# Attention and feed-forward layers in pairs of blocks, with the probabilities divided ahead of the value matmuls

## The reference, cut to what matters

```
x = attn_layer(shift_tokens(x), Wqkv[i], ...) + x      # 16 heads of 64
x = ffn_layer(shift_tokens(x), ...) + x                # 128 -> 2 * 341 -> 128
```

## Time and profile before

| | us |
|---|---|
| median of 3 runs | 1887.88 |
| lowest and highest run | 1884.1, 1891.57 |
| the profiled execution's own time | 1885.08 |
| its span in the trace | 1882.9 |
| TensorE busy (matmul) | 1716.6 (91%) |
| VectorE busy | 1664.4 (88%) |
| ScalarE busy | 1363.7 (72%) |
| GpSimd busy | 1289.6 (68%) |

### The profile page before, as it was taken

The page is one execution under the profiler, slowest core; times in us unless marked ns, Lnnn a source line. Parts: engine busy times, 40 slices in busy tenths (PEclk is TensorE's granted clock), DMA queues, the critical chain, the costliest instruction groups (busy, mean ns, idle before and its releaser), DMA issues. The chain is left out here.

```text
span 1882.9 us, 83647 instructions
## 1 busy us (share of the span) xinstructions
PE 1716.6 (91%) x33456; PEld 1329.2 (71%) x33456; DVE 1664.4 (88%) x3697; ACT 1363.7 (72%) x2647; POOL 1289.6 (68%) x724
## 2 busy tenths in 40 slices
PE   3947899999999999999999999999999999999984
PEld 2524677777777777777777777777777777777773
DVE  5788889999999999899999899999899999999975
ACT  3334678777777877877777787787777778778762
POOL 1538767777767777777777677777677777777741
PEclk8878999999999999999999999999999999999996
DMA  3001222222322222322212322222321222222220
GB/s 133 1 1 46 81 69 58 53 67 78 91 65 67 54 58 78 102 54 67 67 48 75 111 53 59 67 60 62 111 65 49 64 67 68 66 67 59 53 68 23
DMA packets 80680, 121.62 MB, mean 65 GB/s; under 512 B 16776, under 2 KB 29574, under 8 KB 79750
## 3 DMA queue, kind: packets, MB, share of 16 engines
q1 hardware_dynamic: 80646, 121.14, 24.1%
HBM read 19.36 MB, written 1.05 MB: 11 GB/s over the span
## 5 line engine op out<-in xcount | busy, mean ns | idle before, releaser
L1174 POOL TENSOR_TENSOR rot<-rot,root 128x1024 f32<-128x1024 f32 x192 | 365.3, 1903 | 392.3 <-DVE root L1048 392.3
L716 PE MATMUL r<-wqkv,xs 128*128 (+1 forms) x1152 | 528.6, 595 | 5.3 <-ACT xs L879 3.9
L1159 POOL TENSOR_TENSOR rot<-rot,rot_sin 128x1024 f32<-128x1024 f32 x192 | 451.2, 2373 | 0.0
L902 ACT ACTIVATE squares<-r 128x512 f32<-128x512 f32 x384 | 229.0, 597 | 298.1 <-PE r L716 295.2
L716 PEld LDWEIGHTS r<-wqkv,xs 128*128 128x128 f32 x1152 | 205.0, 191 | 194.6 <-issue 187.2
L1010 DVE TENSOR_TENSOR rot_sin<-r,table 128x512 f32<-128x512 f32 x384 | 245.3, 679 | 0.0
L1005 DVE TENSOR_TENSOR rot<-r,table 128x1024 f32<-128x1024 f32 x192 | 234.0, 1219 | 12.5 <-ACT squares L902 8.4
L1166 POOL TENSOR_TENSOR squares<-squares 128x512 f32<-128x512 f32 x192 | 241.6, 1281 | 0.6 <-ACT squares L902 0.4
L721 PE MATMUL r<-square,rot 128*128 128x128 f32 x1536 | 206.0, 279 | 36.1 <-DVE rot_sin L1010 30.4
L1179 POOL TENSOR_TENSOR sm<-sm,rowmax 128x1024 f32<-128x1024 f32 x96 | 182.6, 1902 | 65.7 <-DVE rowmax L1058 65.7
L721 PEld LDWEIGHTS r<-square,rot 128*128 128x128 f32 x1536 | 172.0, 143 | 58.5 <-DVE rot_sin L1010 50.8
(11 more groups left out here) (131 smaller groups left out, 3165.1 us busy)
## 6 DMA issues: line engine op xcount, KB each, us to landing
vwin<-vtok SPq DMA_DIRECT2D x576, 128.0 KB
vwin<-vtok SPq DMA_DIRECT2D x384, 64.0 KB
wqkv<-in_wqkv SPq DMA_DIRECT2D x6, 1536.0 KB, 6.3
wo<-in_wo SPq DMA_DIRECT2D x6, 512.0 KB, 3.9
w<-in_w SPq DMA_DIRECT2D x6, 341.0 KB, 3.0
x<-in_x SPq DMA_DIRECT2D x4, 256.0 KB, 3.7
rope<-in_rope SPq DMA_DIRECT2D x1, 1024.0 KB
out_x<-y SPq DMA_DIRECT2D x4, 256.0 KB, 2.3
```

The source lines that it names most:

```text
L716: pe.matmul(dst[:, c * 512:(c + 1) * 512], xs1[:, u, 0:P], w.rearrange("p a n -> p (a n)"), start=True, stop=True).then_inc(S[done], 1)
L902: last = act.activation(squares[:, k, c * 512:(c + 1) * 512], src[:, c * 512:(c + 1) * 512], ACT.Square)
L1159: pool.tensor_tensor(r, r, rot_sin[:, k, :, :, :].rearrange("p h a d -> p h (a d)"), ALU.add)\
L1174: pool.tensor_tensor(r, r, bcast(root[:, k * HEADS:(k + 1) * HEADS], 2, DH), ALU.mult)\
```

## The change

A step now takes a pair of blocks, m = 0 to 47, and each engine's order within a step is new.

- Four blocks of values are kept in `vtok`, and `vwin`, `qT`, `sm`, `probs`, `rinv` and `pT` have a copy for the even and the odd block.
- `find_roots` serves a pair: 64 sums of squares, one column that is only filler, and two variances, 67 columns; the first operation works on 65.
- VectorE divides the probabilities (`weigh`) ahead of their transposition. In `attend` the values are stationary (64 rows, 64 columns) and the probabilities move (32 columns); the result has features on partitions, so ScalarE copies it straight into `attnT`. The eight transpositions and the division of the attended values are gone.
- Output projection, centring, norm, gate and down projection work on 256 tokens. The up projection comes in three pieces, one for each part of the 341 rows, placed apart in the orders. The variance and the spreading of its root take two matmuls a pair each.
- The first residual is written by one operation into a tile of its own, `mid`, with a column of zeros ahead of each sequence; ScalarE makes the shifted copy `xs2` from it (`stage2`, two operations). `xT` has such a column as well, and the carried columns are gone.
- ScalarE loads the tables for GELU and for the exponential once a pair.
- On SyncE the loads of `w1` and `w2` come after all four spreadings at a layer's end, that of `wo` ahead of them.

The diff, cut to its core. In `step` of TensorE the waits that guard the reuse of PSUM are left out; ScalarE's step is left out.

```diff
+PAIRS = STEPS // 2
+PPL = NB // 2
+PPB = BPB // 2
+W2 = 2 * P
...
-ROOTS = 2 * HEADS + 1
+QK_ROOTS = 4 * HEADS
+ROOTS = QK_ROOTS + 3
...
+        ss = sb("ss", [P, QK_ROOTS + 1])
+        qT = sb("qT", [P, 2, FT, P])
+        vtok = sb("vtok", [P, 4 * INNER])
+        vwin = sb("vwin", [P, 2, NW, FT, DH])
+        sm = sb("sm", [P, 2, HEADS, 2 * WIN])
+        probs = sb("probs", [P, 2, HEADS, 2 * WIN])
+        rinv = sb("rinv", [P, 2, HEADS])
+        pT = sb("pT", [P, 2, FT, P])
+        attnT = sb("attnT", [P, FT, W2])
+        mid = sb("mid", [P, BATCH * (SEQ + 1)])
+        xc = sb("xc", [P, 3, W2])
+        gate = sb("gate", [P, 3, W2])
+        hid = sb("hid", [P, 3, W2])
...
+        LAG, FILLED, BEHIND = 2, 6, 4
...
+            for m in range(FILLED):
+                step(m)
+            with eng.Fori(FILLED, PAIRS) as m:
+                step(m)
+            for m in range(PAIRS, PAIRS + BEHIND):
+                step(m)
...
+                pairs = sp.snap(PPL * (layer + 1))
+                pieces = sp.snap(3 * PPL * (layer + 1))
+                following = sp.snap(layer + 1)
+                sp.wait_ge(S["wo_done"], pairs)
+                weights.load_wo(sp, following)
                 spread_v(used, 0)
-                sp.wait_ge(S["wo_done"], used)
-                weights.load_wo(sp, layer + 1)
                 spread_v(used + 1, 1)
                 spread_v(used + 2, 0)
-                sp.wait_ge(S["up_done"], used)
-                weights.load_w1(sp, layer + 1)
                 spread_v(used + 3, 1)
-                sp.wait_ge(S["down_done"], used)
-                weights.load_w2(sp, layer + 1)
+                sp.wait_ge(S["up_done"], pieces)
+                weights.load_w1(sp, following)
+                sp.wait_ge(S["down_done"], pairs)
+                weights.load_w2(sp, following)
             with sp.Fori((STEPS - NB) // 2 + 2, STEPS // 2) as j:
...
+            def turn_probs(n, u, dst):
+                pe.wait_ge(S["weighted"], n + 1)
+                transpose_all(dst, probs[:, u, :, :].rearrange("p h k -> p (h k)"), "pT_done")
...
+            def attend(n, u, dst):
                 pe.wait_ge(S["pT_copied"], n + 1)
+                pe.wait_ge(S[f"v_spread{u}"], SPREADS * (n // 2 + 1))
                 pe.sem_inc(S["attend_begun"], 1)
                 for i in range(FT // 2):
+                    for w in range(NW):
+                        for s in range(2):
+                            for e in range(2):
+                                half = slice(2 * WIN * e, 2 * WIN * (e + 1))
                                 rows = slice(WIN * w, WIN * (w + 1))
+                                at = 512 * e + P * i
+                                last = pe.matmul(dst[DH * s:DH * (s + 1), at + WIN * w:at + WIN * (w + 1)],
+                                                 vwin[half, u, w, 2 * i + s, :],
+                                                 pT[half, u, (FT // 2) * s + i, rows], start=True, stop=True)
+                last.then_inc(S["attended"], 1)
...
+            def out_project(m):
+                pe.wait_ge(S["attnT_copied"], 2 * (m + 1))
+                pe.wait_ge(S["wo_loaded"], 16 * (m // PPL + 1))
                 for f in range(FT):
+                    last = pe.matmul(pm_out[:, 0:W2], wo[:, f, :], attnT[:, (f % 2) * (FT // 2) + f // 2, :],
+                                     start=(f == 0), stop=(f == FT - 1))
                 last.then_inc(S["wo_done"], 1)
...
+            def ff_up(m, t, dst):
+                if t == 0:
+                    pe.wait_ge(S["xn2_ready"], m + 1)
+                    pe.wait_ge(S["w1_loaded"], 16 * (m // PPL + 1))
+                at, rows = FFT[t]
                 for half in range(2):
+                    last = pe.matmul(dst[0:rows, half * W2:(half + 1) * W2],
+                                     w1[:, half * FF + at:half * FF + at + rows], xn2[:, :], start=True, stop=True)
                 last.then_inc(S["up_done"], 1)
...
+            def step(m):
+                if runs(m - 2):
+                    attend(2 * m - 4, 0, r1)
+                if runs(m - 4):
+                    ff_up(m - 4, 1, pm_out)
+                if runs(m):
+                    project(2 * m, 0, 1, r0, "k_proj")
+                if runs(m - 3):
+                    spread_rstd(m - 3)
+                if runs(m - 1):
+                    turn_k(2 * m - 2, 0, r1)
+                if runs(m - 2):
+                    turn_probs(2 * m - 3, 1, r2)
+                if runs(m - 4):
+                    pe.wait_ge(S["gated"], 3 * (m - 4) + 2)
+                    ff_up(m - 4, 2, pm_out)
+                if runs(m - 1):
+                    pe.wait_ge(S["kT_copied"], 2 * m - 1)
+                    turn_q(2 * m - 2, 0, r1)
+                if runs(m - 2):
+                    attend(2 * m - 3, 1, r2)
+                if runs(m - 1):
+                    score(2 * m - 2, 0, r1)
+                if runs(m):
+                    pe.wait_ge(S["k_turned"], 3 * (2 * m + 1))
+                    project(2 * m, 0, 0, r0, "q_proj")
+                if runs(m - 1):
+                    turn_k(2 * m - 1, 1, r2)
+                if runs(m - 2):
+                    out_project(m - 2)
+                if runs(m - 1):
+                    pe.wait_ge(S["kT_copied"], 2 * m)
+                    turn_q(2 * m - 1, 1, r2)
+                if runs(m):
+                    pe.wait_ge(S["q_turned"], 3 * (2 * m + 1))
+                    project(2 * m + 1, 1, 0, r0, "q_proj")
+                if runs(m - 1):
+                    pe.wait_ge(S["masked"], 2 * m - 1)
+                    score(2 * m - 1, 1, r1)
+                if runs(m):
+                    project(2 * m + 1, 1, 1, r2, "k_proj")
+                    project(2 * m, 0, 2, r1, "v_proj")
+                if runs(m - 4):
+                    ff_down(m - 4)
+                if runs(m - 2):
+                    ff_center(m - 2)
+                if runs(m - 1):
+                    turn_probs(2 * m - 2, 0, r1)
+                if runs(m):
+                    pe.wait_ge(S["q_turned"], 3 * (2 * m + 2))
+                    project(2 * m + 1, 1, 2, r0, "v_proj")
+                if runs(m - 2):
+                    ff_var(m - 2)
+                if runs(m - 3):
+                    ff_up(m - 3, 0, r2)
...
+            def find_roots(m):
+                before = ROOT_OPS * m
+                if runs(m):
+                    dve.wait_ge(S["q_summed"], 2 * (m + 1))
+                    dve.wait_ge(S["k_summed"], 2 * (m + 1))
+                    dve.tensor_scalar(minus_half[:, 0:QK_ROOTS + 1], ss[:, :],
                                       1e-24, -0.5, ALU.max, ALU.mult)\
+                       .then_inc(S["refined"], 1 if runs(m - LAG) else 2)
+                if runs(m - LAG):
+                    dve.wait_ge(S["var_done"], m - LAG + 1)
+                    dve.tensor_scalar(minus_half[:, QK_ROOTS + 1:ROOTS], pm_norm[:, 0:2], 1e-5, -0.5, ALU.add, ALU.mult)\
+                       .then_inc(S["refined"], 1 if runs(m) else 2)
                 dve.wait_ge(S["refined"], before + 2)
+                if runs(m - 1):
+                    dve.wait_ge(S["q_scaled"], 2 * m)
+                    dve.wait_ge(S["k_scaled"], 2 * m)
+                if runs(m - LAG - 1):
+                    dve.wait_ge(S["rstd_spread"], m - LAG)
                 dve.tensor_scalar(root[:, :].bitcast(I32), minus_half[:, :].bitcast(I32), -0.5, GUESS,
                                   ALU.mult, ALU.add).then_inc(S["refined"], 1)
...
+            def weigh(n, u):
                 dve.wait_ge(S["inverted"], n + 1)
...
+            def residual1(m):
+                dve.wait_ge(S["wo_done"], m + 1)
+                at = pair_at(m) + 1
+                dve.tensor_tensor(mid[:, bass.ds(at, W2)], pm_out[:, 0:W2], xT[:, bass.ds(at, W2)], ALU.add)\
+                   .then_inc(S["residual1"], 1)
...
+            def step(m):
+                if runs(m - 1) or runs(m - 3):
+                    find_roots(m - 1)
+                if runs(m - 2):
+                    sums(2 * m - 3, 1)
+                if runs(m - 4):
+                    ff_gate(m - 4, 0, r2)
+                if runs(m - 2):
+                    weigh(2 * m - 3, 1)
+                if runs(m - 4):
+                    ff_gate(m - 4, 1, pm_out)
+                if runs(m):
+                    tables(2 * m, 0)
+                    turn_cos(2 * m, 0, 1, r0, "k_squared", "k_turned", "kT_done")
+                    turn_sin(2 * m, 0, 1, r0, "k_turned", "k_added")
+                    norm_square(2 * m, 0, 1, "k_folded", "k_summed")
+                if runs(m - 3):
+                    ff_norm(m - 3)
+                if runs(m - 1):
+                    mask(2 * m - 2, 0, r1)
+                if runs(m - 4):
+                    ff_gate(m - 4, 2, pm_out)
+                if runs(m - 1):
+                    largest(2 * m - 2, 0)
+                if runs(m):
```

(61 more changed lines are left out.)

740 lines of the change are left out of this document (398 added, 342 removed).

## The result

The changed kernel takes 1905.84 us (median of 4 runs, 1904.78 to 1907.27), the kernel before 1888.31 beside it: a ratio of 1.0097 with a 95% interval of [1.0084, 1.0111], so 1% slower. The forecast was 1841, 2.5% faster, with a range to 1900. The profiled execution took 1907.27 us, 68.9 more than the sum of 1838.4.

What follows compares the result with a forecast made beforehand. VectorE and GpSimd waiting on each other were to bound it, TensorE just under: 162.8 outside the layers + 48 x 33.2 (1593.6) + 57 fill and drain + 25 layer changes = 1838, plus 2.8 for the median: 1841 us, range 1770 to 1900.

Steps and rivals of the forecast that it cites:

- the sum of 1838.4: Profiled execution: 162.8 us outside the layers, 1593.6 for 48 pairs, 57 for fill and drain, 25 for layer changes.
- The pair (T = 33.2): Steady time of one pair of blocks: 33.2 us, where it was 34.84.
- Attend, taken at 2.1: Attend on TensorE, 1.49 us before: more columns loaded, fewer streamed, so 2.1, with ends 1.5 and 3.0.
- The ring of VectorE and GpSimd: Main forecast: these two engines' waits on each other set the pair, TensorE just under; chance 0.52, 1810 to 1870 us.
- the walk: New order traced through one pair on VectorE and GpSimd with operation lengths and waits, giving 32.7 us.
- the 0.5 added for misses: Added to the pair's 32.7 us because the engines' orders mesh closely, giving 33.2.
- the first product wait: Root chain on VectorE: first product of two SBUF tiles waits for GpSimd's last add, from 28.6 until 30.4 us.
- Layer changes ... 2.3 + 0.4 + 6.4, and 2.3 to land ... 5 are lost each, 25 in all: Five layer changes: copies queued on SyncE land after 11.4 us, TensorE stands 6 to 7 at attend, some 5 lost.
- Ends: fill and drain ... 57: Start and end of the layers: 90 us for a pair through five steps, less one pair: 57, ends 40 and 80.
- no change: Rival: one more wait for a whole GpSimd operation makes a pair 34.2 us, total 1887; chance 0.11.
- The slower rival, attend's loads: Attend's weight loads bind TensorE once attend passes 2.6 us; at 3.0 the time is 1928, at 3.6 1985; chance 0.15.
- the rule that the prediction names from the Trainium skill: On TensorE a weight load overlaps running matmuls only if its row group differs; would put attend at 3.0 or 3.6 us.

Runs made afterwards that it cites:

- FILLED 10: The changed kernel with the first 10 steps written out ahead of the loop, not 6: 1919.98 us.
- FILLED 5: The changed kernel with blocks 4 and 5's copies issued before SyncE's wait, plus five steps written out ahead of the loop, not six: 1845.31 us.
- its three corrections: The changed kernel with early copies, first root operation reading 5 groups and writing 80 columns, and five steps written out: 1828.75 us, 0.9686 of the kernel before.

## Why the prediction was wrong

Point by point, by its own steps.

- **The pair (T = 33.2) held**: 33.27. Attend, taken at 2.1 between 1.5 and 3.0, is 2.0 to 2.07. Passes of the output projection are 0.216 (0.213). GpSimd is busy 79% (about 80). The ring of VectorE and GpSimd sets T, as the third refinement left out (0.79 less) and half of attend (only 0.5 less) show. With half of attend the pair takes 32.79, near the 32.7 of the walk, so the 0.5 added for misses had the right size; it was a guess. Table means 1.40 us (over 1.2 expected). The division means 1.34, not near 1.6: it waits less than I walked.
- **One detail of the ring was wrong, without a price**: I had the first product wait, as an operation with two tiles of SBUF. The chain's first operation, of one source, waited already. As both end with the add, T came out alike, which is partly luck; what would help is another thing, the shape of that operation.
- **"Layer changes ... 2.3 + 0.4 + 6.4, and 2.3 to land ... 5 are lost each, 25 in all"** is the step that failed first. The 0.4 is what SyncE needs to issue the load of wqkv, and I treated the load as done. Its row on the page of the kernel before had the real figure, not among the rows that I took:

```profile
wqkv<-in_wqkv SPq DMA_DIRECT2D x6, 1536.0 KB, 6.3
```

  The copies behind it land 5.65 us after their issue, not 2.3; TensorE waits 11.1 to 11.3 at four changes, not 6 to 7, and 6.5 at the fifth, which has no such load. And the full wait and more is lost (12.7 us at the change shown), not 5 of 6 to 7, with the clock at 0.50 behind it. Measured 59 for 25. The place, the number of waits (five) and the order in the queue were right, only the size was off: with the copies ahead of the wait 54.5 us come back, with the load behind them the wait is 6.3 as forecast.
- **"Ends: fill and drain ... 57"** failed second: 89. The part that I estimated, 90 for one pair passing through less one T, was right (39.6 + 49.9, less 33.3). What failed is that the sum gives the steps ahead of the steady loop the same T as all others: the first six intervals take 28 us more, the last 3. FILLED 10 and FILLED 5 put 3.5 and 6.0 us on one body of code that runs for the first time; for six of them that is 21 to 36, which covers the 28. But half of attend, with as many steps written out, has 9 only, so the price depends on what TensorE has in a step, and the waits and the clock of the first steps (0.93 granted over the six intervals) weren't measured by themselves. So the cause of this second error is shown only in part.
- **The rivals.** None described the outcome. By its size it belongs with "no change", chance 0.11, but that rival had T at 34.2, and T is 33.27. (Its sum of 1887 leaves out the 2.8 that the others have: 1890.) The slower rival, attend's loads, didn't happen: 2.07 us, not over 2.6. Attend was not at the upper prices of the rule that the prediction names from the Trainium skill ("TensorE: Matmul & The Clock Gate", The mechanism); and with all loads on one half first, where that rule should cost most, attend takes 2.46, so the trace bears it out in its direction and not in its size for tiles of 64 x 64.
- **The sum and the range.** The forecast's own mechanism, with two small terms too small, crossed to the other side: the 48 pairs save 75 us (34.84 less 33.27 each), while fill, drain and layer changes grow from 50 to 148, 98 more; the rest, 22, is the result (1907.3 against 1885.1 in the profiled executions). The upper end of 1900 was taken from rivals about T. Fill and drain had a bound of 80, the layer changes had no upper bound at all, and both came out higher.

Not tried: `minus_half`, `root_t` and `rinv` in PSUM. The old division, with one side in PSUM, took 1.23 us, and the chain and the new division might no longer wait for GpSimd. The four PSUM tiles of the layers are all in use, and TensorE would write beside them, so what it would bring stays open. What the division alone loses to GpSimd, and GpSimd to it, wasn't isolated either.

## What to carry to other kernels

A term of a few microseconds that comes five times deserves the same care as one that comes 48 times. Ask of each queue what a wait in it holds up, and price a transfer that starts behind a large one by that one's landing, not by its issue; issue a copy that an engine needs soon ahead of any wait that it doesn't depend on. Keep steps in the loop where conditions allow it, and price those outside it by their own rows. Try a change of an order once with its late transfers moved ahead before it is judged: this one was 1.0% slower as made, and 3.1% faster with its three corrections.

## What was not expected of the hardware

- Copies of 64 and 128 KB within SBUF landed 2.0 to 2.3 us after their issue by themselves, and the last of ten landed 5.65 us after its issue beside a load of 1.5 MB, with the DMA share at 1.01.
- After 11.3 us of idling TensorE was granted 0.50 in the 5 us from 572; behind the wait of 6.3 us attend took the same 3.64 us.
- An operation of VectorE with one source and 64 or 65 columns took 1.79 us beside a GpSimd add; with outer sizes of 5 and 80 it took 0.235.
- Steps written out once cost 3.5 to 6 us more than the same steps in a loop, with TensorE idle for 0.7 to 3.3 us at a time, often in the middle of a run of matmuls. The first pass through the loop cost as much. The DMA queue for instructions moved packets in just these stretches, and none in the later passes.
